# Relation edge stage of a two-layer graph network: the score split, the one-hot, the mask and PE's wait rearranged

## The reference

```python
att = (q[edge_dst] * key_e).sum(-1) * rel_pri[edge_type] / jnp.sqrt(jnp.float32(dk))
seg = edge_dst * r + edge_type
amax = jax.ops.segment_max(att, seg, num_segments=S)
ex = jnp.exp(att - amax[seg])
denom = jax.ops.segment_sum(ex, seg, num_segments=S)
w = ex / denom[seg]
hsum = jax.ops.segment_sum(w[:, :, None] * val_e, seg, num_segments=S)
```

## Time and profile before

| what | value |
|---|---|
| median of 3 runs | 4414.78 us (4411.69 to 4416.05) |
| profiled execution | 4411.88 us |
| its span, first to last instruction | 4410.1 us |
| PE busy in the span | 3737.7 us (85%) |
| DVE | 3896.1 us (88%) |
| ACT | 2905.2 us (66%) |
| POOL | 3339.3 us (76%) |

### The profile page before, as it was taken

The page is one execution under the profiler, slowest core; times in us unless marked ns, Lnnn a source line. Parts: engine busy times, 40 slices in busy tenths (PEclk is TensorE's granted clock), DMA queues, the critical chain, the costliest instruction groups (busy, mean ns, idle before and its releaser), DMA issues. The chain is left out here.

```text
span 4410.1 us, 111708 instructions
## 1 busy us (share of the span) xinstructions
PE 3737.7 (85%) x21988; PEld 3075.1 (70%) x21989; DVE 3896.1 (88%) x12732; ACT 2905.2 (66%) x8431; POOL 3339.3 (76%) x3789
## 2 busy tenths in 40 slices
PE   4978888888888886997888998898888989986776
PEld 3557777777777775886677777776776777765775
DVE  7879999999999996554899999999999998986887
ACT  3845555555555553443888888888888888884333
POOL 3668888888888884443888888888888888883665
PEclk8989999999999998999888888888889888887999
DMA  3778878887877775665777777777777777775553
GB/s 119 221 227 229 228 230 227 229 228 227 229 227 229 229 227 130 236 237 206 206 206 204 205 205 206 204 205 205 206 205 205 204 204 206 205 194 163 175 175 124
DMA packets 579324, 907.10 MB, mean 206 GB/s; under 512 B 213896, under 2 KB 407480, under 8 KB 578728
## 3 DMA queue, kind: packets, MB, share of 16 engines
q0 software_dynamic: 169984, 585.34, 46.7%
q1 hardware_dynamic: 409256, 320.86, 25.4%
HBM read 734.08 MB, written 175.09 MB: 206 GB/s over the span
## 5 line engine op out<-in xcount | busy, mean ns | idle before, releaser
L1541 POOL DMA_INDIRECT kv1c<-kv_table,rec x936 | 916.8, 979 | 259.3 <-issue 181.2
L893 POOL DMA_INDIRECT kv<-kv_table,rec x864 | 920.9, 1066 | 248.5 <-issue 229.7
L1595 ACT ACTIVATE wv<-kv1c,wv 128x64 f32<-128x64 f32 x3744 | 927.8, 334 | 2.2
L1673 DVE CUSTOM_DVE_ANT_0 masked_scores<-score_p,mask 126x384 f32<-126x384 f32 x1248 | 679.5, 545 | 9.7 <-issue 5.5
L1771 PE MATMUL sum_p<-wv,hot 128*126 128x260 f32 x1872 | 617.0, 476 | 1.9 <-ACT wv L1595 1.9
L1060 PE MATMUL sum_p<-msg,hot 128*126 128x256 f32 x1728 | 431.8, 393 | 193.3 <-DVE msg L1016 193.3
L1733 PE MATMUL qe_p<-qrel,hotT 126*128 126x256 f32 x1872 | 541.2, 432 | 22.6 <-ACT hotT L1573 16.3
L1530 POOL TENSOR_SCALAR hot<-iota,local 128x126 f32<-128x126 f32 x936 | 549.2, 600 | 0.2 <-issue 0.2
L1060 PEld LDWEIGHTS sum_p<-msg,hot 128*126 128x126 f32 x1728 | 308.1, 188 | 281.3 <-DVE msg L1016 214.1
L1733 PEld LDWEIGHTS qe_p<-qrel,hotT 126*128 126x128 f32 x1872 | 424.6, 227 | 107.8 <-ACT hotT L1573 16.5
L930 ACT ACTIVATE attn_act<-attn 128x4 f32<-128x4 f32 x216 | 44.4, 206 | 647.7 <-DVE attn L994 647.7
(11 more groups left out here) (274 smaller groups left out, 9013.9 us busy)
## 6 DMA issues: line engine op xcount, KB each, us to landing
key<-segment_keys SPq DMA_DIRECT2D x312, 189.0 KB
q_blk<-q_table SPq DMA_DIRECT2D x216, 192.5 KB, 3.6
acc_table<-acc SPq DMA_DIRECT2D x312, 128.0 KB
qrel<-q_by_relation SPq DMA_DIRECT2D x312, 126.0 KB
feat<-in_edge_feat_t SPq DMA_DIRECT2D x216, 128.0 KB, 3.7
agg_and_x_plus_h<-total SPq DMA_DIRECT2D x216, 126.0 KB
kv1c<-kv_table,rec POOLq DMA_INDIRECT x936
kv<-kv_table,rec POOLq DMA_INDIRECT x864
```

Of the source, the lines that this page charges most:

```text
L893: pool.indirect_dma_start(kv[k][:, t, :], None, c["kv0_d"], bass.IndirectOffsetOnAxis(ap=rec[k][:, t, 0:1].bitcast(I32), axis=0)).then_inc ...
L1541: pool.indirect_dma_start(kv[k][:, t, :], None, c["kv1_d"], bass.IndirectOffsetOnAxis(ap=rec[k][:, t, 0:1].bitcast(I32), axis=0)).then_inc ...
L1595: ins = act.activation(wv[k][:, t, h, 0:DK], kv[s][:, t, D + h * DK:D + (h + 1) * DK], ACT.Copy, scale=wv[k][:, t, h, DK:DK + 1])
L1673: dve.tensor_tensor_reduce(junk[k][:, h, :], score_p[:, h, :], mask[it.slot(4)][:], 1.0, -BIG, ALU.add, ALU.max, top[s][:, h:h + 1]).then_ ...
```

## The change

Within `edges_1`:

- The transposed parts get lanes: each of the three tiles of 128 edges has its 12 part rows in a lane of 32 columns, so that one transpose of 96 columns takes the place of three of 12; the spread's weights are loaded three times, once per lane, and its matmuls read partitions 0, 32 and 64.
- `dist` becomes `far` = |BIG * (key - segment)| (a parameter is scaled on the host). `hotT` = relu(1 - far/BIG); the maxima take score minus `far`. `mask` goes.
- The one-hot is made on DVE in one instruction; `local` goes.
- The split moves to POOL, between `faded` and the gathers.
- PE multiplies two constant tiles six times a chunk, ahead of the turn; nothing reads the result.
- `cap` and `old_peak` use a two-tensor form instead of a tensor and a scalar.
- ACT's and DVE's lists are reordered; ACT's fade has a place of its own.

The diff, cut to its core:

```diff
-        spread_head = sb("spread_head", [HEADS * PARTS, HEADS, SEG], BF16)
+        LANE = 32
+        spread_head = sb("spread_head", [T1 * LANE, HEADS, SEG], BF16)
+        WARM = 6
+        ones = sb("warm_ones", [P, D], BF16)
-        parts = [sb(f"score_parts{k}", [P, T1, PARTS, HEADS], BF16) for k in range(2)]
+        parts = [sb(f"score_parts{k}", [P, T1, LANE], BF16) for k in range(2)]
-        score_p = ps("score_p", [SEG, HEADS, CH1])
+        score_p = ps("score_p", [SEG, T1, HEADS, P])
@@ sync
+                for t in range(T1):
+                    sp.dma_start(spread_head[t * LANE:t * LANE + PARTS * HEADS, :, :], w0["spread_head"]
@@ gpsimd
-                def one_hot(it):
...
+                def split_scores(it):
+                    k, n = it.slot(2), it.slot(4)
+                    hold(pool, held, score_ready, it.count())
+                    wait(pool, partsT_turned, it, 2)
+                    pool.tensor_copy(part(k, 0), score[n][:]).then_inc(split_ready, 1)
+                    pool.wait_ge(split_ready, it.count(1, 4, 1))
+                    pool.tensor_tensor(rest[k][:], score[n][:], part(k, 0), ALU.subtract).then_inc(split_ready, 1)
+                    hold(pool, held, split_ready, it.count(1, 4, 2))
+                    pool.tensor_copy(part(k, 1), rest[k][:]).then_inc(split_ready, 1)
+                    pool.wait_ge(split_ready, it.count(1, 4, 3))
+                    pool.tensor_tensor(part(k, 2), rest[k][:], part(k, 1), ALU.subtract).then_inc(split_ready, 1)
-                run_chunks(pool, steps, ((5, fade_acc), (1, one_hot), (0, gather)))
+                run_chunks(pool, steps, ((5, fade_acc), (2, split_scores), (0, gather)))
@@ scalar
+                    wait(act, top_ready, it, 4, per=HEADS)
+                    act.activation(far[k][:], key[s][:].rearrange("s (p t) -> s t p", t=T1), ACT.Abs,
+                                   bias=par[s][0:SEG, 0:1], scale=BIG).then_inc(far_ready, 1)
-                def masks(it):
...
-                run_chunks(act, steps, ((1, transposed_hot), (2, masks), (0, distances), (4, weights), (2, partsT_out)))
+                run_chunks(act, steps, ((4, weights), (4, weigh), (2, partsT_out), (0, distances), (0, transposed_hot),
+                                        (4, fades)))
@@ vector
+                def one_hot(it):
+                    wait_slot(dve, loaded, it, LOADS)
+                    wait(dve, summed, it, U)
+                    dve.scalar_tensor_tensor(hot[s][:],
+                                             c["iota"][:].rearrange("p (o n) -> p o n", o=1).to_broadcast([P, T1, SEG]),
+                                             par[s][:, 1:2], rec[s][:, :, 2:3].to_broadcast([P, T1, SEG]),
+                                             ALU.add, ALU.is_equal).then_inc(hot_ready, 1)
+                    for h in range(HEADS):
+                        dve.tensor_tensor_reduce(junk[k][:, h], score_p[:, :, h, :], far[it.slot(4)][:], 1.0, -BIG,
+                                                 ALU.subtract, ALU.max, top[s][:, h:h + 1]).then_inc(top_ready, 1)
+                    dve.tensor_tensor(old[s][:], peak[it.prev().slot(U)][:],
+                                      par[s][0:SEG, 2:3].to_broadcast([SEG, HEADS]), ALU.add).then_inc(old_ready, 1)
+                    dve.tensor_tensor(capped[it.slot(2)][:], diff[it.slot(2)][:], zeros[:],
-                run_chunks(dve, steps, ((2, q_times_k), (4, below_peak), (2, scores), (4, cap), (0, locate),
...
+                run_chunks(dve, steps, ((2, q_times_k), (3, old_peak), (4, below_peak), (2, scores), (4, cap),
+                                        (3, maxima), (5, add_acc), (3, new_peak), (0, one_hot), (3, peak_drop)))
@@ tensor
+                def keep_warm(it):
+                    wait(pe, partsT_ready, it, 1)
+                    for _ in range(WARM):
+                        pe.matmul(warm_p, identity[:], ones[:], start=True, stop=True)
+                    pe.transpose(partsT_p, parts[k][:].rearrange("p t c -> p (t c)"),
+                                 identity[:]).then_inc(partsT_turned, 1)
+                            rows = slice(t * LANE, t * LANE + PARTS * HEADS)
+                            ins = pe.matmul(score_p[:, t, h, :], spread_head[rows, h, :], partsT[k][rows, :],
-                run_chunks(pe, steps, ((5, sum_values), (1, q_of_edges), (2, turn_parts), (3, peaks_of_edges),
+                run_chunks(pe, steps, ((5, sum_values), (1, q_of_edges), (2, keep_warm), (2, turn_parts), (3, peaks_of_edges),
                                        (2, spread)))
```

More of the change, by code:

```diff
@@ L1521, in _ @@
             def _(pool):
-                pool.wait_ge(filled, U + 1)
+                pool.wait_ge(filled, FILLS)
                 steps = chunk_steps(pool, c["steps1"])
-                def one_hot(it):
[L1526 to L1532, removed]
                 def gather(it):
@@ L1587, in weights, with weigh @@
                     act.activation(wv[k][:, :, :, DK], capped[k][:], ACT.Exp).then_inc(weight_ready, 1)
-                    wait(act, drop_ready, it)
-                    wait(act, faded_ready, it, U)
-                    act.activation(fade[s][:], drop[s][:], ACT.Exp).then_inc(fade_ready, 1)
+                def weigh(it):
+                    k, s = it.slot(2), it.slot(U)
                     wait(act, weight_ready, it)
@@ L1597, in weights, with fades @@
                     ins.then_inc(wv_ready, 1)
+                def fades(it):
+                    s = it.slot(U)
+                    wait(act, drop_ready, it)
+                    wait(act, faded_ready, it, U)
+                    act.activation(fade[s][:], drop[s][:], ACT.Exp).then_inc(fade_ready, 1)
                 def partsT_out(it):
@@ L1610, in _ @@
                     dve.memset(acc[k][:], 0.0).then_inc(filled, 1)
+                dve.memset(zeros[:], 0.0).then_inc(filled, 1)
+                for k in range(2):
+                    dve.memset(parts[k][:], 0.0).then_inc(filled, 1)
+                dve.memset(ones[:], 1.0).then_inc(filled, 1)
                 dve.tensor_copy(identity[:], c["ident"][:]).then_inc(filled, 1)
-                dve.wait_ge(filled, U + 1)
+                dve.wait_ge(filled, FILLS)
                 steps = chunk_steps(dve, c["steps1"])
-                def locate(it):
+                def one_hot(it):
                     s = it.slot(U)
                     wait_slot(dve, loaded, it, LOADS)
-                    wait(dve, hot_ready, it, 2)
-                    dve.tensor_scalar(local[it.slot(2)][:], rec[s][:, :, 2], par[s][:, 1:2], None,
-                                      ALU.subtract).then_inc(local_ready, 1)
+                    wait(dve, summed, it, U)
[3 more added lines that the diff above has]
+                                             ALU.add, ALU.is_equal).then_inc(hot_ready, 1)
                 def q_times_k(it):
@@ L1707, in cap @@
                     wait(dve, weight_ready, it, 2)
-                    dve.tensor_scalar(capped[it.slot(2)][:], diff[it.slot(2)][:], 0.0, None,
+                    dve.tensor_tensor(capped[it.slot(2)][:], diff[it.slot(2)][:], zeros[:],
                                       ALU.min).then_inc(capped_ready, 1)
```

120 lines of the change are left out of this document (39 added, 81 removed).

## The result

The changed kernel takes 4460.91 us (median of 4 runs, 4457.8 to 4464.66) against 4413.37 us for the kernel before on the same chip (4 runs): ratio 1.0111, 95% interval 1.0098 to 1.0123. It is slower by 1.1%, outside the range given. Its profiled span is 4461.9 us.

A forecast was written before the change was run, and what follows sets the result against it. POOL was taken as the bound at 6.09 us a chunk, falling to 5.65 = 0.60 + 1.24 + 0.16 + 3.57 + 0.08; over 312 chunks, less 1 us once, 136 us saved: 4279 us, range 4150 to 4385.

The forecast's parts named there:

- What bounds the kernel now: Relation edge stage: POOL never rests, 6.09 us of work a chunk in a period of 6.09; DVE close behind at 6.08.
- POOL's sum: POOL's work per chunk after the change: `faded`, split, gap, gathers and contention, 5.65 us instead of 6.09.
- The split: Four small operations on POOL before the gathers: subtractions 0.20 us, copies 0.15, waits 0.18 each, 1.24 us a chunk.
- DVE's sum: DVE's work per chunk after the change: 5.21 us instead of 6.08, with the maxima 0.49 us apart.
- One-hot: One DVE instruction of 378 elements replaces POOL's three: 0.46 us to the next start, bounds 0.40 and 0.60.
- `capped`: DVE operation of 12 elements in two-input form: about 0.12 us start to start instead of 0.56, lasting near 0.16.
- The loop: Score, split, gather, landing and `qk`: 11.1 us for two periods, 5.6 each; just misses being the bound.
- The first (cheap small operations): POOL's small operations take 0.1 us each, POOL falls to 4.9, period 5.25: 4153 us; chance 15%.
- The fourth: Slower: the split in POOL's queue delays every gather; 6.6 us a chunk, 4438 us, at the upper bound 4915; chance 11%.
- the third: PE's clock is not held, or the six matmuls are in the way: PE's 5.4 us grows to 5.9, 4355 us; 10%.
- The rule against it: Two-input DVE instructions and SBUF-reading POOL instructions exclude each other; the trace disagreed for short ones, left the long one open.
- The full second rival: DVE and POOL shut each other out: one-hot holds a gather back by 0.46 us, POOL 6.03, 4396 us; chance 8%.

The follow-up runs named there:

- split_dve_late_b: Changed kernel with the split woven between DVE's maxima again and SP's store one period later: 4179.31 us, 0.9466 of the kernel before.
- fade_between: Changed kernel with POOL's order as split, `faded`, gather instead of `faded`, split, gather: 4601.88 us, 1.0099 of the kernel before.
- cover: Changed kernel plus one independent POOL operation of 126 columns between the split and the first gather: 4587.3 us, 1.0050 of the kernel before.
- group 3: Runs sharing one chip, where the kernel before took 4508 us; changed kernel there 4545.03 us, without the six matmuls 4490.68 us.
- group 4: Four late-store kernels sharing one chip, where the kernel before took 4417.28 us; with the late store alone it took 4414.84 us.

## Why the prediction was wrong

**What bounds the kernel now**: right. POOL was the bound before and still is, and its sum of parts gives the period both times.

**The step that failed** is POOL's sum, "0.60 + 1.24 + 0.16 + 3.57 + 0.08 = 5.65 us", and in it the 0.16 us of idle time ahead of the first gather, which came to 0.62 in the chunk shown and 0.63 on average. Term by term, from start to start; the means are over the middle 1200 us, 196 chunks before and 191 after:

| term | before, mean | predicted | after, the chunk shown | after, mean |
|---|---|---|---|---|
| `faded` | 0.60 | 0.60 | 0.57 | 0.58 |
| `hot` before, split after | 1.76 | 1.24 | 1.35 | 1.37 |
| gap ahead of the first gather | 0.16 | 0.16 | 0.62 | 0.63 |
| gathers, with contention | 3.57 | 3.65 | 3.74 | 3.67 |
| sum | 6.09 | 5.65 | 6.28 | 6.25 |

So POOL gave up 1.76 + 0.16 = 1.92 us and took on 1.37 + 0.63 = 2.00, and its gathers grew by 0.10. The kernel missed the forecast by 182 us (4460.91 against 4279); 0.47 x 312 = 147 of them are the one gap, and the split's 0.13 is another 41. I had written that these gaps "belong to the price" of a gather, and carried 0.16 over to a place behind another, shorter operation. In the earlier trace rows the last of three `hot` starts near 3007.91 (3006.74 and two thirds of 1.76), and the gather 0.75 us behind it. After the change the gather starts 0.83 us behind the start of the last split operation (3007.45 to 3008.28), which lasts 0.21 and not 0.59. In split_dve_late_b `faded`, 0.62 long, starts at 3003.74 and the gather at 3004.57, 0.83 again. Behind `faded` in fade_between it is 0.84 in 131 of 180 chunks, behind the cover 0.70 in 110 of 183. A case inside the changed kernel itself, first POOL's timeline, then DVE's:

```profile
2627.49 0.55 POOL L1566 TENSOR_TENSOR score_parts<-score_rest,score_parts 128x12 bf16<-128x12 f32 x1 [0.18 <-POOL score_parts L1563]
2628.32 1.00 POOL L1537 DMA_INDIRECT kv1c<-kv_table,rec  x1 [0.28 <-issue]
...
2627.36 0.61 DVE L1635 SCALAR_TENSOR_TENSOR hot<-iota,par,rec 128x378 f32<-128x378 f32 x1
```

Here the last split operation took 0.55 instead of 0.21, and the gather still started 0.83 us behind its start. The measure is start to start, hardly moved by the length of the operation ahead. Why it is 0.70 or 0.75 behind one operation and 0.83 behind another the runs don't tell.

**The other terms.** The split: operations of 0.19 to 0.21 us with 0.18 between, as the slope of the earlier trace rows gave them for subtractions (0.20); the copies are no cheaper (0.15 taken). DVE's sum: 5.21 predicted, 5.09 measured without its waits, the maxima 0.48 apart (0.49). One-hot: 0.53 to the next start (0.46). `capped`: mean 351 ns, not 0.16; in the kernel before its mean was 359, so the new form gained nothing, and 0.44 us of saving was read off one chunk. The loop: with the true terms 11.1 + 0.46 + 0.11 + 0.09 = 11.8 us for two periods, 5.9 each; it stays under 6.28, so it "just misses being the bound", as said. (The 2.05 in the 11.1 is 1.94 by the earlier trace rows: 3003.68 to 3005.62.)

**The rivals.** The first (cheap small operations) fell on the split's 1.35 us. The fourth had the right place, POOL's queue ahead of the gathers, and the right sign, but decided "from a split chain of 1.7 us on": the chain was 1.35 and the gap behind it 0.62, together more than 1.76 + 0.16. Its figure of 4438 us doesn't follow from its own 6.6 us a chunk: 0.51 x 312 on top of 4415 gives 4574. That 4438 lies near the 4461 measured is chance. I had priced the operations and not what they stop covering. Of the third, both halves show, though POOL's full row means that they don't set the period in the first profile: the clock still falls to 0.50 at times, and the six matmuls are in the way when it does. PE's timeline at the upper clock:

```profile
3012.43 0.82 PE L1728 MATMUL turn_p<-warm_ones,ident_bf 128*128 128x256 bf16 x6
```

as predicted (0.8). But in the chunk before, still partly at 0.50 (granted clock 0.60 from 3003 to 3006 us), the six run from 3007.75 and the turn starts at 3008.41, 0.75 us after the split's end at 3007.66. That the versions without the six came to 0.9916, 0.9957 and 0.9970, and 1.2% under the changed kernel in the group that ran both, fits, and there the wait for the score accounts for the whole difference (68.6 against 13.7 us). In the profile of the changed kernel where the prediction was made that wait is 1.9 us of 1200, so there the six can have cost little in this way. That they lengthen the wait by delaying the turn is read from the trace, not isolated.

**The rule against it.** The first gather takes 1.23 us when DVE's one-hot (3008.03 to 3008.63) covers its start, against 0.95 for the others. Over 2400 to 3600 us the first gather takes 1.18 on average in the 126 chunks where the one-hot runs at its start, and 1.00 in the other 66. The POOL operation stretched to 0.55 above ends at 2628.04, the one-hot at 2627.97; the 15 split operations that began beside a one-hot average 0.53 us for 0.20. This last is what the Trainium skill, SBUF — State Buffer, section Who interferes with whom, says of a DVE instruction with two SBUF inputs against a GpSimd instruction that reads SBUF, and I had given it too little. For the gathers the order matters: in split_dve_late_b a gather from 3005.85 to 3006.81 lasts 0.96 with the one-hot starting at 3006.41, and neither is stretched; 219 gathers there in which a one-hot starts average 0.955, and 15 that start during a one-hot 1.17. `capped` at 3005.50 lasts until 3005.79, the gather beside it until 3005.74; but in the 49 chunks in which `capped` runs beside a gather and is done before `faded` it keeps its 0.16, so not the whole of a gather stretches it. The size of 0.08 for the one-hot against the gather was about right: the first gather takes 1.115 us on average, 0.12 over the undisturbed one and 0.07 over its 1.042 in the kernel before. Split operations beside the maxima keep their 0.2 us. The full second rival, 0.46 of contention a chunk, didn't come; over the kernel before the gathers cost 0.10 more, and that is more than half of the 0.16 by which the period grew.

## What to carry to other kernels

The idle time ahead of an indirect DMA is a property of the pair, the DMA and the operation ahead of it: take it from start to start (here 0.7 to 1.0 us), and when a short operation replaces a long one ahead of a gather, count what it no longer covers. Four small dependent operations cost 0.31 us woven between long ones on DVE and 1.8 us on POOL: count a chain with its waits on the engine where it lands. When an engine is relieved, look which load or store comes next in a queue that was just in time; the later store gave nothing by itself (0.9998) where the kernel before takes 4417 us. It is part of the version that reached 0.9466; that version without it was run only where the kernel before takes 4505 us and more, and there it waits 109 to 167 us for its loads.

## What the runs showed that I had not expected

- In the changed kernel and in cover and fade_between the first gather of a chunk starts, all but a few times, 0.70 to 0.98 us behind the start of the POOL operation ahead of it, whether that lasts 0.21, 0.40, 0.55 or 0.62 us.
- A gather that starts while DVE's one-hot runs ends a fixed time after the one-hot does: 0.87 us in 117 of 126 cases of the changed kernel's first profile, 0.82 in the 15 of split_dve_late_b. One in which a one-hot starts is not stretched. The second and third of a group keep 0.30 us behind the end of a gather 0.95 long.
- The spread's 12 matmuls, in three lanes of 32 rows, take 0.44 us at the upper clock where they took 0.90:

```profile
3009.34 0.44 PE L1744 MATMUL score_p<-score_partsT,spread_head 12*126 12x128 bf16 x12
```

- The six constant matmuls lift the stage's granted clock from 0.82 to 0.88 (group 3) and from 0.88 to 0.98 (group 4), without a gain in either.
- The same kernel takes 4417 us in one group and 4505 to 4557 us in the others, and an edit's worth differs with it: split on DVE with the late store is 0.9466 in group 4 and 0.9753 in group 3. The chip's number in the record doesn't separate them.
